# Retention layer: row variance and inverse root one step sooner, squares on ScalarE, transposes ahead of the output product

## What is computed

```python
x = x + _L0_attn_ref(_layernorm(x), ...)
x = x + _L0_xattn_ref(_layernorm(x), ctx, ctx, ...)
x = x + _L0_ffn_ref(_layernorm(x), ...)      # attention, then experts
x = x + _L1_attn_ref(_layernorm(x), ...)     # retention
x = x + _L1_xattn_ref(_layernorm(x), ctx, ctx, ...)
x = x + _L1_ffn_ref(_layernorm(x), ...)      # experts
```

```python
Q, K, V = x @ WQ, x @ WK, x @ WV             # by head
Q, K = xpos_rotate(Q), xpos_rotate(K)        # pairs of columns turned by position
QKD = (Q @ K.T) * D                          # D: decay by distance, causal, one per head
R = QKD @ V
mu, var = mean(R), var(R)                    # by row and head
Rn = (R - mu) * rsqrt(var + 1e-5) * gamma + beta
y = Rn @ WO
```

## Time and profile before

| | us |
|---|---|
| runs | 1399.4 median of 3 (1397.3 to 1399.57) |
| profiled execution | 1399.71, its span 1397.9 |
| busy in the span | TensorE 1265.2, VectorE 837.1, GpSimd 625.7, ScalarE 570.2 |
| retention's steps | about 936 to 1054 of the span |

### The profile page before, as it was taken

One profiled execution on the slowest core, in us unless ns is written; L12 is line 12 of the kernel. 1 busy time (PEld: TensorE's weight loads), 2 busy tenths in 40 slices (PEclk: granted clock), 3 DMA queues, 4 the chain that ended last, 5 costly groups with the idle time before them and its releaser, 6 DMA issues.

```text
span 1397.9 us, 35660 instructions
## 1 busy us (share of the span) xinstructions
PE 1265.2 (91%) x13189; PEld 1061.5 (76%) x13189; DVE 837.1 (60%) x2007; ACT 570.2 (41%) x1272; POOL 625.7 (45%) x853
## 2 busy tenths in 40 slices
PE   5999989989999999989999999959998999938997
PEld 4767758977777788768899999947776788727886
DVE  3887834347888777756521121259975678783446
ACT  2555545424444555652222222224543445523331
POOL 4455531035565355530233333238783444427536
PEclk9999979989999999999999999989998999968999
DMA  7000000020000000000489999641000001027954
GB/s 271 3 2 0 2 31 1 1 94 17 14 15 3 6 18 11 17 16 16 183 313 322 352 322 324 225 143 32 1 17 9 25 24 31 17 73 262 400 195 147
DMA packets 47440, 138.14 MB, mean 99 GB/s; under 512 B 6958, under 2 KB 29679, under 8 KB 41137
## 3 DMA queue, kind: packets, MB, share of 16 engines
q1 hardware_dynamic: 33008, 110.64, 22.3%
q0 software_dynamic: 7536, 19.67, 4.0%
q10 hardware_dynamic: 6768, 6.16, 1.3%
HBM read 119.80 MB, written 17.83 MB: 98 GB/s over the span
## 4 chain that ended last, share of the span: by engine, by line
PE 56%; DVE 20%; issue 9%; POOL 7%; DMA 5%; ACT 2%; DVEq 0%; POOLq 0%; SPq 0%; ACTq 0%
PE ps L1120 11%; PE ps L1354 10%; PE ps L1038 8%; DVE negmax L1783 6%; PE ps L1366 5%; PE ps L1082 4%; DMA row_in<-rows_of,from_u 4%; PE ps L1062 3%; PE ps L983 3%; PE ps L986 2%; PE ps L924 2%; PE ps L1089 2%; PE ps L999 1%; PE ps L971 1%; DVE u L1762 1%
## 5 line engine op out<-in xcount | busy, mean ns | idle before, releaser
L1420 ACT ACTIVATE probsT_all<-ps 128x1024 f32<-128x1024 f32 x128 | 131.2, 1025 | 161.3 <-PE ps L986 161.3
L1783 DVE TENSOR_REDUCE negmax<-ps 128x8 f32<-128x1024 f32 x128 | 155.8, 1217 | 61.7 <-PE ps L983 61.4
L1354 PE MATMUL ps<-hT,w_tile 128*128 128x128 f32 x1304 | 161.5, 278 | 0.8 <-DMA w_tile<-in_w_f 0.6
L1354 PEld LDWEIGHTS ps<-hT,w_tile 128*128 128x128 f32 x1304 | 153.4, 193 | 3.2 <-issue 1.6
L986 PE MATMUL ps<-qe,kf 32*128 32x256 f32 x1280 | 151.9, 385 | 0.0
L983 PE MATMUL ps<-kf,qe 32*128 32x128 f32 x2048 | 148.5, 284 | 0.0
L983 PEld LDWEIGHTS ps<-kf,qe 32*128 32x128 f32 x2048 | 129.7, 190 | 1.9 <-issue 1.2
L986 PEld LDWEIGHTS ps<-qe,kf 32*128 32x128 f32 x1280 | 109.5, 187 | 3.9 <-issue 2.7
L2345 DVE TENSOR_TENSOR h_in<-ps,act_sb 128x512 f32<-128x512 f32 x39 | 27.0, 692 | 136.5 <-PE ps L1354 136.5
L1413 ACT ACTIVATE hT<-ps,vecs 128x128 f32<-128x128 f32 x142 | 47.2, 385 | 141.6 <-PE ps L1339 129.2
L701 POOL DMA_INDIRECT back_of<-be,to_u x39 | 39.4, 1010 | 137.0 <-DVE be L2358 137.0
(11 more groups left out here) (284 smaller groups left out, 3228.2 us busy)
## 6 DMA issues: line engine op xcount, KB each, us to landing
w_tile<-in_w_f SPq DMA_DIRECT2D x29, 1536.0 KB, 9.3
w_tile<-in_w_f SPq DMA_DIRECT2D x47, 385.0 KB, 7.0
y_back<-in_w_f SPq DMA_DIRECT2D x10, 1536.0 KB, 8.5
back_of<-w_odd ACTq DMA_DIRECT2D x47, 128.0 KB
ctxT<-in_ctxT SPq DMA_DIRECT2D x32, 128.0 KB, 2.1
rows_of<-nv SPq DMA_DIRECT2D x32, 128.0 KB, 1.7
w_even<-in_w_att SPq DMA_DIRECT2D x3, 1024.0 KB, 6.7
y_back<-back_of SPq DMA_DIRECT2D x6, 512.0 KB, 5.6
```

Of the source, the lines that this page charges most:

```text
L1354: last = mm(ps[:, 2 * which + at.two, fc * P:(fc + 1) * P], w[:, col:col + P], rowT[:, at.two, c, :], start=c == 0, stop=c == KC - 1)
L1420: nc.scalar.activation(half_of(probsT_all, half), ps[:, 2:4].rearrange("p b n -> p (b n)"), ACT.Exp, scale=HD ** -0.5).then_inc(S["probs"], 1)
L1783: nc.vector.tensor_reduce(m, ps[:, 0:2].rearrange("p b (h k) -> p (b h) k", h=HB), AX.X, ALU.max, negate=True).then_inc(S["s_max"], 1)
```

## The change

On VectorE, in RET's steps, the variance is no longer that of the tile at +3 but of the tile at +4 (`ahead`), after the combine and the normalise of the tile at +3; only the first step of RET, which has no tile at -1, also makes the variance of +3. `head_norm` comes behind both, ahead of the swap. GpSimd makes the inverse root of the tile at +4 in the same step, behind the rotary products and ahead of the head power. The first step of XATT1 finds variance and root made. The squares of o are made by ScalarE from PSUM, right after the copy of o, and go into the same gsq; VectorE only sums them. On TensorE `turn_in` goes ahead of `out_project`.

```diff
+    def ahead(self):
+        p, q = (self.p + 1) % 2, (self.q + 1) % 4
+        if isinstance(self.t, int) and self.t + 1 == NT:
+            return Tile(self.l + 1, 0, p, q)
+        return Tile(self.l, self.t + 1, p, q)
...
             def step(at):                                   # GpSimd
-                if 3 in at and not first_crossed(at[3]) and not (at[3].l == RET and isinstance(at[3].t, int) and at[3].t == 2):
+                rooted = -1 in at and at[-1].l == RET
+                if 3 in at and not rooted and not first_crossed(at[3]) and not (at[3].l == RET and isinstance(at[3].t, int) and at[3].t == 2):
                     inverse_root(at[3], at[3].p)
...
                 norm_low(normed(at))
+                if 0 in at and at[0].l == RET:
+                    inverse_root(at[3].ahead(), at[3].ahead().p)
                 if -1 in at and at[-1].l == RET:
                     tile = at[-1]
                     wait_apart(pool, ("gn_var", reached("gn_var", tile)))
...
                         project_values(at[1])               # TensorE
+                    if 3 in at:
+                        turn_in(at[3], at)
                     if late:
                         out_project(late, at)
-                    if 3 in at:
-                        turn_in(at[3], at)
...
                     wait(act, "oT_out", tile.back(2))       # ScalarE, attended
-                    copy(o[:, tile.p].rearrange("p (h d) -> p h d", h=H),
-                         ps[:, B_O, 0:H * VW].rearrange("p (h d) -> p h d", h=H)[:, :, 0:HD]).then_inc(S["o_sb"], 1)
+                    src = ps[:, B_O, 0:H * VW].rearrange("p (h d) -> p h d", h=H)[:, :, 0:HD]
+                    copy(o[:, tile.p].rearrange("p (h d) -> p h d", h=H), src).then_inc(S["o_sb"], 1)
+                    if tile.back(1).l == RET:
+                        wait(act, "gn_var", tile.back(1))
+                    nc.scalar.activation(gsq.rearrange("p (h d) -> p h d", h=H), src, ACT.Square).then_inc(S["o_sb"], 1)
...
                     wait(dve, "o_sb", tile)                 # VectorE, attended
-                    link(tt(gsq, o[:, p], o[:, p], ALU.mult), 1)
                     nc.vector.tensor_reduce(gn[:, p, 0], gsq.rearrange("p (h d) -> p h d", h=H), AX.X,
...
                 to_max = at[1] if 1 in at and at[1].l != RET else None     # VectorE, late_step
-                if 3 in at:
+                if not out:
                     variance(at[3])
                 combine_next(at)
+                normalise(at[3])
+                variance(at[3].ahead())
                 if late:
                     head_norm(late)
-                if 3 in at:
-                    normalise(at[3])
                 if 2 in at:
                     swap(at[2])
...
                 first = rooted(at)                          # VectorE, step
-                if first and not first_crossed(first[0]):
+                if first and not first_crossed(first[0]) and not (out and out.l == RET):
                     variance(first[0])
```

More of the change, by code:

```diff
@@ L161 @@
         "gn_eps": (RET,), "gn_rstd": (RET,), "nm_sb": SOFTMAX, "m_out": SOFTMAX, "inj_sb": SOFTMAX,
-        "o_sb": (RET,), "rotated": ROTARY}
+        "rotated": ROTARY}
 PER_TILE = {"s_out": (2, 2, 2, 0, 2), "s_max": (2, 2, 2, 0, 2), "st_out": (2,) * 5, "probs": (2,) * 5, "pv_out": (2,) * 5,
             "dve_ln": (1, 1, 1, 1, 1), "dve_nm": (4, 1, 1, 0, 1),
-            "dve_o": (2, 1, 1, 1, 1), "pool_r": (2, 1, 2, 1, 1), "pool_m": (0, 2, 0, 2, 0)}
+            "o_sb": (0, 0, 0, 2, 0), "dve_o": (2, 1, 1, 0, 1), "pool_r": (2, 1, 2, 1, 1), "pool_m": (0, 2, 0, 2, 0)}
 N_PER_TILE = {"lg_out": (0, 1, 1), "lg_sb": (0, 1, 1), "n_base": (2, 1, 1), "n_sq": (0, 1, 0)}
```

## The result

| | changed kernel | kernel before |
|---|---|---|
| first comparison, median of 14 runs each | 1402.7 us | 1398.05 us |
| second comparison (after_again), 12 and 35 runs | 1402.9 us | 1399.4 us |

A forecast was written before the change was run, and what follows sets the result against it. Equally long GpSimd and TensorE loops (7.57 and 7.58 us) were taken to bound the retention steps. Start +1.1, middle +2.7, end -0.4, next layer -0.8 and clock -3.8 gave -1.2 on 1399.7: 1398.5 us, range 1395.0 to 1403.5.

The forecast's parts named there:

- Two loops of 7.57 and 7.58: Retention step before the change: a GpSimd loop of 7.57 us and a TensorE loop of 7.58 us, equally long.
- The step of 7.83: Retention loop after the change: 7.45 plus GpSimd's root caught 0.17 and power 0.21 by VectorE; 11 loops cost +2.7 us.
- Start, +1.1: First retention steps: 0.66 us for a second variance, 0.45 for a second step of 8.02 instead of 7.57.
- Transposes, nothing: Transposes ahead of TensorE's output product: worth zero, since turn_in waits for the same oT; the 0.52 gap stays.
- End of retention, -0.4: Last two retention steps: output product no longer waits for value rows, squares gone; -0.4 us, between 0 and -0.8.
- First step of the next layer, -0.8: L1882 no longer held 1.09 us by a GpSimd product; reduction, L1762 and maximum follow sooner: -0.8 us.
- Clock, -3.8: Half-clock stretch behind retention, likelier than not, does not come as TensorE's gaps shrink: -3.8 us, bounds 0 and -5.
- Rival A: The clock behind retention falls all the same, nothing repays the longer loop: +2.6, 1402.3 us; chance 0.27.
- C: GpSimd's power shuts VectorE out, so L1762 waits for its end: loop 8.8, 1409 us; chance 0.03.
- B: GpSimd's root and power are not caught by VectorE; TensorE's 7.58 stands: -4.3, 1395.4 us; chance 0.13.
- D: Head power off the path, gap filled, 7.1 us a step, no loss at the start: 1389.7 us; chance 0.04.

The follow-up runs named there:

- after_again: The changed kernel run once more with no edit, against the kernel before: ratio 1.0032 (1.0015 to 1.0049), median 1402.9 us.
- product_before: The kernel before with GpSimd's head power replaced by a product of the same shape (head norms then wrong): 7.58 us a step, now and then 7.65.
- before_look_2: The kernel before, unchanged, in its third profiled execution: 1395.3 us.
- squares_only: The kernel before with only the squares (L1882) moved to ScalarE: ratio 0.9994 (0.9978 to 1.0011), swaps 7.64 us apart.
- after_late_turn: The changed kernel with turn_in back behind out_project: ratio to the kernel before 1.0034 (1.0018 to 1.0050), swaps 7.83 us apart.
- product_after: The changed kernel with GpSimd's head power replaced by a product of the same shape (head norms then wrong): 7.36 us a step, now and then 7.44.
- transposes_only: The kernel before with only turn_in moved ahead of out_project in the retention steps: ratio 1.0004 (0.9984 to 1.0024), swaps 7.57 us apart.
- variance_only: The changed kernel with squares back on VectorE and turn_in behind out_project: ratio to the kernel before 1.0002 (0.9984 to 1.0019), swaps 7.57 us apart.

## Why the prediction was right or wrong

- *Two loops of 7.57 and 7.58*: right. The TensorE loop showed itself by itself in product_before (7.58).
- *The step of 7.83*: right in cause, and in size with some luck. Measured 7.83 to 7.84; the last two steps 7.76 for 7.79. s5-s15 grew by 2.41. The root was caught for 0.27 where I had 0.17 (0.83 for 0.56) and the power for 0.13 where I had 0.21 (3.04 for 2.91), because the second rotary product led to L768 in 1.05 and not in 1.17; the errors cancel to a hundredth. The collisions, as far as they lengthen the step, need both parts of the change: 7.57 with the variance alone, and 7.64, by one collision of the power, with the squares alone.
- *Start, +1.1*: s1-s2 grew by 0.76 for 0.66, s3-s5 by 0.75 for 0.45 + 0.26. Missed is s2-s3, 8.64 and 7.72, where the kernel before has 6.48 twice and 8.04 once. With the second variance TensorE waits 2.16 ahead of its first weighing, 1.40 before, and the projection behind it ran at half clock (3.79 for 2.05), so that the swap waited 2.98 for it. The first row is VectorE, the others TensorE, in the changed kernel:

```profile
941.37 0.01 DVE L1874 LOAD_MASK_SELECT qk_swap<-qk_raw  x1 [2.98 <-ACT qk_raw L1422]
...
934.72 2.12 PE L1092 MATMUL ps<-probsT_all,va 128*32 128x128 f32 x32 [2.16 <-DVE probsT_all L1789]
936.77 3.79 PE L1048 MATMUL ps<-hT,w_odd 128*128 128x128 f32 x16
```

  and in before_look_2, without the second variance:

```profile
936.22 0.65 PE L1082 MATMUL ps<-probsT_all,va 128*32 128x128 f32 x16 [1.40 <-DVE probsT_all L1776]
...
938.27 3.18 PE L1038 MATMUL ps<-hT,w_odd 128*128 128x128 f32 x16
```

  But whether this stretch comes is mostly settled ahead of the change. The projection that starts 0.4 behind s1 in every kernel, ahead of all that the edits move, ran at full clock in before_look_2 and in part at half clock in the first execution of the kernel before:

```profile
928.55 2.05 PE L1038 MATMUL ps<-hT,w_odd 128*128 128x128 f32 x16 [0.76 <-ACT hT L1412]
```

```profile
930.31 2.76 PE L1038 MATMUL ps<-hT,w_odd 128*128 128x128 f32 x16 [2.47 <-ACT hT L1412]
```

  It took 2.05 in 8 of the 20 profiled executions, both of the changed kernel and two with VectorE's old order (before_look_2, squares_only) among them, and all 8 have a stretch at half clock behind the first weighing (s2-s3 of 7.72 to 8.65). In the other 12 it took 2.76 to 3.78, and only 2 of them, after_late_turn and product_after, have the stretch (8.06). By the means of the table s2-s3 is +1.2; that this is the change's isn't shown, since two executions of one kernel and three of the other happened to come in different states.
- *Transposes, nothing*: right in result as far as runs can tell (1.0004 alone; 1.0034 without them beside 1.0032 to 1.0034 with them), wrong in its reason. I took the releaser that the row names for the one that decides. The output product waits for va, turn_in doesn't, and TensorE's loop became 7.36. It was worth nothing in the steps because GpSimd's loop, 7.57 before and 7.83 after, was the longer one.
- *End of retention, -0.4*: wrong in size: 0.0 in the first execution (20.85 for 20.84) and +1.4 in the second (22.20). The squares alone gave 0.9 there; the new order took it back. The first head norm behind s15 starts 0.07 behind a GpSimd product and takes 1.25 for 0.42, and TensorE stands idle for 1.75 ahead of the transposes of o; its longest gap there was 0.99 before. In after_again half clock followed at once (1.68 for 1.03), in the first execution it didn't:

```profile
1049.02 1.04 POOL L789 TENSOR_TENSOR qe<-qf,const 128x512 f32<-128x512 f32 x1
1049.09 1.25 DVE L1917 TENSOR_TENSOR o<-o,gn 128x256 f32<-128x256 f32 x1 [2.20 <-POOL gn L899]
1050.40 0.44 PE L1023 MATMUL ps<-const,o 128*128 128x128 f32 x2 [1.75 <-DVE o L1917]
1050.67 1.68 PE L1063 MATMUL ps<-w_odd,hT 128*128 128x256 f32 x4
```

- *First step of the next layer, -0.8*: right, 19.36 for 20.20 and 20.21, which is 0.85.
- *Clock, -3.8*: the step that failed. I read a stretch at half clock as a property of the kernel before. It had been a matter of one execution: mask to maximum was 23.64 there and 20.20 and 20.21 in the two others, and 20.21 in transposes_only and variance_only. The changed kernel had nothing to win there against the median. My sum was made against that one execution. There the term was nearly right (the stretch was gone, worth 3.4), but in the same profile s2-s3 was 2.2 longer and the last part 1.5, which took its worth back. Without the clock term my sum was +2.6.

Put together from the table, against the kernel before without the stretch behind retention, and leaving out what comes and goes with the clock: 0.76 + 0.75 + 2.41 + 0.0 - 0.85 = +3.1. Measured were 4.6, and between 2.1 and 6.9 by the two intervals, so +3.1 lies inside, in the lower half. Stretches at half clock could fill the 1.5 that are left (by the means of the table +1.2 in s2-s3, +0.7 in s15-mask, +1.4 behind the fifth maximum), but five executions don't show how much of that is the change's: it stays open. Rival A's time, 1402.3, was nearly hit, though not by its condition: A had the same stretch stay, while two of the three executions of the kernel before never had it. C is out: u ran its 0.41 inside the power's 3.04, unhindered, and so did the second combine (0.48). The Trainium skill's rule (SBUF — State Buffer, Who interferes with whom) held for products, where L1882 waited for L777's end (1.32 for 0.41), and not for the power. B failed: both collisions came. D is out too, since the head norm waited 1.30 for the power.

## What to carry to other kernels

When two loops are equally long, an edit in one is worth nothing until the other is opened too; find, for each loop, the single instruction that has to stand ahead of what closes it, and put all the rest behind. Here that was the head norm ahead of the swap. With the row norm left in its place and u behind the swap, the squares on ScalarE and the transposes ahead came to 0.3% less time; with the row norm a step sooner the three parts cost 0.3%. Taking work off an engine that isn't late moves everything behind it, and may move it into the other engine's instructions. A term that rests on a slow-clock stretch seen in one profiled execution should be kept out of the sum until a second execution shows it, and two executions should be compared only where the clock ahead was the same.

## What the runs showed of the hardware

- The granted clock of one and the same kernel falls at different places in different executions: three profiled executions of the kernel before differ by 3.4 us behind retention, by 1.6 in one retention step and by up to 2.0 behind the last attention layer. Its 35 runs spread from 1392.7 to 1405.4, and 12 runs beside them left an interval of 0.17% to either side.
- Whether half clock came in one place went with whether it had been there shortly before: at the start of retention 8 of 8 executions in which the projection 0.4 behind s1 ran at full clock (2.05) had a stretch at half clock behind the first weighing, and 2 of the 12 others.
- A power on GpSimd (2.9 us for 128x16) is caught by a VectorE product only around its start, by 0.13 to 0.16 (the 128x1 root by 0.27), and doesn't hold VectorE up for the rest of its length (rotary sums, combine and u at 0.41 to 0.48 inside it). A GpSimd product of 1.0 to 1.2 us does: 1.32 for a square of 0.41, 1.25 for a head norm of 0.42, and 1.12 for a u of 0.41 in the kernel before (at 1041.51, beside L782 from 1041.45).
